# Rounding of the cross-attention tiles spread over ScalarE, VectorE and GpSimd, and started at slots of its own from batch to batch

## Chip, cores and metric

One core of one Trainium2 chip. The metric is the time on the device in microseconds (us) of one launch.

## What is computed

A decoder layer in float32 on 4 batches of 512 tokens, 512 features each: causal attention with 32 query heads and 8 key heads, then a product with a context, then a mixture of experts. Each part has a residual and a layer norm ahead of it. The change is in the second part. There the normalised tokens and the context are rounded to fp8 steps before they are multiplied:

```python
xb = x.reshape(E, M, K // BLK, BLK)            # BLK = 128, here per batch of 512 tokens
amax = jnp.max(jnp.abs(xb), axis=-1, keepdims=True)
safe = jnp.maximum(amax, ACT_EPS)
q = (xb * (FP8_MAX / safe)).astype(jnp.float8_e4m3fn)
xq = q.astype(jnp.float32) * (safe / FP8_MAX)
...
x = x + einsum('emk,enk->emn', xq, wq)         # wq: the context, rounded in blocks of 128 x 128
x = x + shared_ffn(layernorm(x)) + chosen_expert(layernorm(x))
```

## The kernel before

Tokens lie in SBUF as 16 tiles `X[:, t, :]` of 128 tokens by 512 features, four tiles (i = 0 to 3) for each batch b. Products in float32 are made of three matmuls of split operands (`three`, L474 to L476: high by high, high by low, low by high), so nearly every tile that is multiplied is first turned on TensorE (PE; `turn_tile`, L466), copied by ScalarE (ACT; L928) and completed by VectorE (DVE; L1312).

The program has three stages. Attention ends at about 1050 us of the span. The stage from there to about 1317 us is the shared feed-forward network, in 8 half batches x of 256 tokens, each cut into 8 parts k:

- parts 0 to 4 are 24 matmuls of 256 columns (`Uh`, `Ul`), part 5 is 12 of them. After each, ACT applies Silu (L971), DVE multiplies (L1441), and the product is split by ACT (`h_hi`, L958) and DVE (`h_lo`, L1428, L1430);
- part 6 is 30 matmuls of 512 columns (`Dh`, `Dl`), part 7 is 4 of them. Part 6 needs the split products of parts 0 to 4, part 7 that of part 5.

The last stage is the eight experts, with the same parts.

The cross part of batches 1 to 3 and the choice of experts run beside the second stage. `slots()` gives every step a slot; every engine walks the same slots, and ahead of part k of half batch x it runs its share of slot 8x + k - 5. For batch b, s = 16(b - 1), and slot s is the one before part 5 of half batch 2(b - 1). Every engine is a queue in program order: what stands behind a waiting instruction waits too. The steps, before the change, with their slots:

- `stats2` (s - 13 + i) and `norm2` (s - 7): mean, variance and reciprocal root on DVE; `rstd_of` is 11 small operations, L1103 to L1114.
- `cross_round` (s - 1 + i), all on DVE for one tile: normalise X into a tile of `T1` (L1127), largest magnitudes of its four blocks (L1301), the scales (L1232 to L1237), the scaling (L1241), the rounding step (L1247, L1249). GpSimd (POOL) then adds the step, subtracts it, and scales back (L1659, L1661, L1663).
- `cross_turn` (s + 1 + i): turn of the rounded tile. `cross_product` (s + 2 + i): 12 matmuls with the context into bank 6, then DVE adds them to X (`cross_add`, L1317).
- `stats3`, `rstd3` (s + 6), `norm3` (s + 7 + i // 2), `route_turn` (s + 9 + i // 2): the third layer norm, from which the half batches 2b and 2b + 1 of the network start at slot s + 11.
- `logits` (s + 12), `choose` (s + 14), `place` (s + 19, for the last batch s + 15): product with the gate weights, the largest logit by a chain of small DVE operations (L1342 to L1361), the places by two small matmuls (L656, L657) and a second DVE chain (L1370 to L1382). Then POOL numbers the tokens (L1720) and sends four indirect DMAs (L1697).

Batch 0 is done during attention; its `logits`, `choose` and `place` stand at slots -4, -2 and 2. The tiles of `T1` and `T2` are pieces of `work` in the profile. `YT` and `XT` hold turned tokens and the turned context.

Of the kernel before, what the change touches and what calls it, by code (L numbers as in the profile page):

```python
# [5 lines left out]
NT, D, NB, TB = 16, 512, 4, 4  # L6
# [4 lines left out]
NU = NG * NB  # L11
# [24 lines left out]
def slots():  # L36

    side = {}


    def plan(s, stage, b, i=0):
        side.setdefault(s, []).append((stage, b, i))

    first = ("route_turn", "cross_turn", "logits", "choose", "place", "cross_product")
    for i in range(TB):
        plan(-36 + i, "context_turn", 0, i)
        plan(-32 + 2 * i, "cross_turn", 0, i)
        plan(-31 + 2 * i, "cross_product", 0, i)
        plan(-30 + 2 * i, "stats3", 0, i)
        plan(-22 + i, "norm3", 0, i)  # L50
        plan(-20 + i, "route_turn", 0, i)
        plan(-16 + i, "context_turn", 1, i)
    plan(-23, "rstd3", 0)
    plan(-4, "logits", 0)
    plan(-2, "choose", 0)
    plan(2, "place", 0)
    for b in range(1, NB):
        s = 16 * (b - 1)
        for i in range(TB):
            plan(s - 13 + i, "stats2", b, i)  # L60
            if b > 1:
                plan(s - 4 + i + i // 3, "context_turn", b, i)
            plan(s - 1 + i, "cross_round", b, i)
            plan(s + 1 + i, "cross_turn", b, i)
            plan(s + 2 + i, "cross_product", b, i)
            plan(s + 3 + i, "stats3", b, i)
            plan(s + 7 + i // 2, "norm3", b, i)
            plan(s + 9 + i // 2, "route_turn", b, i)
        plan(s - 7, "norm2", b)
        plan(s + 6, "rstd3", b)  # L70
        plan(s + 12, "logits", b)
        plan(s + 14, "choose", b)
        plan(s + (19 if b < NB - 1 else 15), "place", b)
    for i in range(2):
        plan(16 * NB - 13 + i, "load_x", i)
        plan(16 * NB - 9 + i, "expert_turn", 0, i)
    plan(16 * NB - 11, "load_slots", 0)

    def place(x):
        return first.index(x[0]) if x[0] in first else len(first) - 9 * (x[0] == "context_turn")  # L80

    for s in side:
        side[s].sort(key=place)
    return side
# [12 lines left out]
def decoder(nc, x_in, ctx_in, wqkv_in, wo_in, wg_in, wf_in, ident_in, mask_in, rope_in, ksin_in, rank_in, tri_in, out):  # L97
# [3 lines left out]
    with ExitStack() as root:  # L101
# [10 lines left out]
        X = sb("X", [128, NT, D])  # L112
# [202 lines left out]
        def tokens(i):  # L315
            return slice(i * 128, (i + 1) * 128)

        def four(y):
            return y.rearrange("p (c n) -> p c n", c=4)
# [7 lines left out]
        def turned_from(x):  # L327
            stage, b, i = x
            if stage == "context_turn":
                return CW[(4 * b + i) % 3]  # L330
            if stage == "cross_turn":
                return T1[(b * TB + i) % 3]
            return XN[:, i, :] if stage == "route_turn" else XE[:, b % 2, i, :]

        def turn_bank(n):
            return 6 if turns[n] in beside else other_at[turns[n]] % 2

        def wait_job_buffer(need, j):

# [441 lines left out]
        def scalar_engine(e):  # L781
            need = Once(e)
# [104 lines left out]
            def look(t):  # L887
# [4 lines left out]
                e.activation(free_wraw[:, 1024:1536], X[:, t, :], ACT.Identity, bias=ssum[:, 0, t:t + 1],  # L892
                             scale=rstd[:, t:t + 1]).then_inc(a_norm, 1)

            def scaled(j):

                y, k = YB[j % 4], job_scales(j, 0)
                if jobs[j][0] == "context":
                    need.wait_ge(v_small, 2)
                    need.wait_ge(d_rb[j % 4], 16 * sum(x[0] == "context" for x in jobs[j % 4:j + 1:4]))  # L900
                else:
                    need.wait_ge(v_small, 4)
                    need.wait_ge(a_norm, TB + jobs[j][1] + 1)
                for c in range(4):
                    last = e.activation(y[:, tokens(c)], y[:, tokens(c)], ACT.Copy, scale=k[:, c:c + 1])
                last.then_inc(a_scaled, 1)
# [23 lines left out]
            def logits(b):  # L930
                need.wait_ge(p_logits, b + 1)
                if b == 0:
                    wait_attention(need)
                else:
                    need.wait_ge(p_lt, b)
                e.activation(LG[:, :], bank[6][:, :], ACT.Copy).then_inc(a_lg, 1)

            def side_slot(s):
                for x in side.get(s, ()):
                    if x in turn_at:  # L940
                        turn(x)
                    elif x[0] == "logits":
                        logits(x[1])

            def split_piece(m, p):
                n = NP * m + p
# [142 lines left out]
        def vector_engine(e):  # L1089
# [3 lines left out]
            def chain(instruction):  # L1093
                own[0] += 1
                instruction.then_inc(v_own, 1)

            def after():
                need.wait_ge(v_own, own[0])
# [17 lines left out]
            def rstd_of(ts):  # L1116
                chain(rstd_first(ts))
                for _ in range(3):
                    rstd_next(ts)
# [6 lines left out]
            def normed(dst, t):  # L1126
                return e.tensor_scalar(dst, X[:, t, :], mv[:, t, 0:1], rstd[:, t:t + 1], ALU.subtract, ALU.mult)  # L1127
# [108 lines left out]
                chain(e.tensor_scalar(r, r, 448.0, None, ALU.mult))  # L1236
                return e.tensor_scalar(d, d, 1.0 / 448.0, None, ALU.mult)  # L1237

            def rounded(n, y, r):
                q = T2[n % 2]  # L1240
                chain(e.tensor_tensor(four(y), four(y), r.unsqueeze(2).to_broadcast([128, 4, 128]), ALU.mult))  # L1241
                after()
                if n < 2:
                    need.wait_ge(p_kv, NU)
                else:
                    need.wait_ge(g_t2, n - 1)
                chain(e.tensor_scalar(q.bitcast(U32), y.bitcast(U32), 0x7F800000, None, ALU.bitwise_and))  # L1247
                after()
                e.tensor_scalar(q, q, 2.0 ** -6, 1.5 * 2.0 ** 20, ALU.max, ALU.mult).then_inc(v_q, 1)  # L1249
# [36 lines left out]
                need.wait_ge(v_bm, j + 1)  # L1286
                e.tensor_scalar(q, q, 2.0 ** -6, 1.5 * 2.0 ** 20, ALU.max, ALU.mult).then_inc(v_bq, 1)

            def cross_round(b, i):
                t = b * TB + i  # L1290
                y = T1[t % 3]
                if b == 1:
                    need.wait_ge(a_kept, len(jobs))
                    need.wait_ge(v_small, 4)
                need.wait_ge(p_turn, turn_at["cross_turn", (t - 3) // TB, (t - 3) % TB] + 1)
                after()
                chain(normed(y, t))
                after()
                if b > 1:
                    need.wait_ge(g_q, round_at["cross_round", b - 1, i] + 1)  # L1300
                chain(e.tensor_reduce(aam[:, i, :], four(y), AX.X, ALU.max, apply_absolute_value=True))  # L1301
                after()
                chain(scales(aam[:, i, :], asc[:, i, 0, :], asc[:, i, 1, :], 1e-4))
                after()
                rounded(round_at["cross_round", b, i], y, asc[:, i, 0, :])

            def turn_lo(x):
                n = turn_at[x]
# [75 lines left out]
            def side_slot(s):  # L1384
                ends = []
                for x in side.get(s, ()):
                    stage, b, i = x
                    if stage == "stats2":
                        need.wait_ge(v_x, last_x(b * TB + i) + 1)
                        stats_of(b * TB + i)  # L1390
                    elif stage == "stats3":
                        need.wait_ge(v_x2, b * TB + i + 1)
                        stats_of(b * TB + i)
                    elif stage in ("norm2", "rstd3"):
                        rstd_of(slice(b * TB, (b + 1) * TB))
                    elif stage == "cross_round":
                        cross_round(b, i)
                    elif stage == "norm3":
                        norm3(b, i)
                    elif stage == "choose":  # L1400
                        choose(b)
                    elif stage == "place":
                        place(b)
                    elif stage == "expert_turn":
                        turn_lo(x)
                    elif stage == "cross_product" or x in turn_at:
                        ends.append(x)
                for x in ends:
                    if x in turn_at:
                        turn_lo(x)  # L1410
                    else:
                        cross_add(x[1], x[2])
# [179 lines left out]
        def gpsimd_engine(e):  # L1592
# [108 lines left out]
            def side_slot(s):  # L1701
                for x in side.get(s, ()):
                    stage, b, i = x
                    if stage == "cross_round":
                        rounded(round_at[x], T1[(b * TB + i) % 3], asc[:, i, 1, :])
                    elif stage == "place":
                        number(b)
                        scatter(b)
# [421 lines left out]
```

## Time and profile before

| | us |
|---|---|
| median of 3 runs (1546.54 to 1547.84) | 1546.98 |
| the profiled execution, its own time | 1547.13 |
| span of its trace | 1545.3 |
| busy: PE, DVE, POOL, ACT | 1444.7, 1166.0, 1025.9, 960.9 |

The span runs from the first to the last instruction; 1.8 us of the execution's own time lie outside it. Busy time is a sum over the whole span, and each stage has its own limit, so what counts is who waits for whom in the stage that is touched. PE is busy 93% of the span on average, and least in the slices of the second stage.

### The profile page before, as it was taken

The page shows a single profiled execution, that of the slowest core. Times are in us where ns is not written, and L with a number is a line of the kernel's source. Part 1 is how long each engine was busy: PE and PEld are TensorE (multiplying, and loading weights), DVE is VectorE, ACT ScalarE, POOL GpSimd, SP SyncE. Part 2 cuts the span into 40 slices and gives each one's busy share as a digit, 9 for nine tenths or more (in the row PEclk, how much of TensorE's full clock was granted, in tenths as well). Part 3 has the DMA queues.
Part 4 walks back from the last instruction along what each step waited for, and adds up shares of the span by engine and source line. Part 5 has one row for each costly group of instructions (what it writes and reads, how often), then busy time and mean ns, then how long its engine had stood idle before and what let it go on. Part 6 is the DMA issues. An engine that isn't in the chain of part 4 may idle for free.

```text
span 1545.3 us, 26936 instructions
## 1 busy us (share of the span) xinstructions
PE 1444.7 (93%) x8617; PEld 1264.8 (82%) x8617; DVE 1166.0 (75%) x2877; ACT 960.9 (62%) x2446; POOL 1025.9 (66%) x1043
## 2 busy tenths in 40 slices
PE   5999999999999999999999999886989899999997
PEld 4778888888878888778888887765888879999996
DVE  7678888888888887778878888786767664677773
ACT  4677777787677787878888788663121212556562
POOL 3787888887886889888889889443403041366663
PEclk9999999999999999999999999998999999999999
DMA  6445444334231433424334333403111010587772
GB/s 209 128 112 174 137 125 137 98 98 120 75 95 49 128 84 97 122 60 120 95 91 133 90 110 93 130 22 124 42 42 42 21 42 34 167 268 230 254 242 84
DMA packets 108620, 174.74 MB, mean 113 GB/s; under 512 B 20936, under 2 KB 42696, under 8 KB 108480
## 3 DMA queue, kind: packets, MB, share of 16 engines
q1 hardware_dynamic: 104448, 160.51, 35.5%
q0 software_dynamic: 3840, 12.25, 2.1%
q8 instruction: 70, 1.15, 0.3%
q14 instruction: 70, 0.57, 0.1%
q10 hardware_dynamic: 192, 0.26, 0.1%
HBM read 94.05 MB, written 33.18 MB: 82 GB/s over the span
## 4 chain that ended last, share of the span: by engine, by line
PE 66%; DVE 13%; ACT 11%; issue 5%; DMA 2%; POOL 1%; SPq 1%; DVEq 0%; POOLq 0%; ACTq 0%
PE bank L474 15%; PE bank L476 14%; PE bank L475 14%; PE bank L526 5%; ACT P L865 5%; PE bank L541 4%; PE bank L542 4%; PE bank L492 4%; PE bank L493 3%; DVE P L1179 2%; ACT PTh L877 2%; PE bank L466 2%; ACT Otmp L871 2%; DVE PTl L1220 1%; DVE Opair L1214 1%
## 5 line engine op out<-in xcount | busy, mean ns | idle before, releaser
L865 ACT ACTIVATE P<-P,mn 128x512 f32<-128x512 f32 (+3 forms) x512 | 284.6, 557 | 206.3 <-DVE mn L1179 202.3
L1616 POOL TENSOR_TENSOR P<-P,ri 128x128 f32<-128x128 f32 (+3 forms) x512 | 360.1, 735 | 31.1 <-DVE ri L1168 30.8
L1179 DVE CUSTOM_DVE_ANT_0 P<-bank,mask 128x512 f32<-128x512 f32 (+3 forms) x512 | 236.8, 481 | 88.8 <-PE bank L493 87.1
L1220 DVE TENSOR_TENSOR PTl<-bank,PTh 128x512 fp32r<-128x512 f32 (+1 forms) x384 | 229.7, 599 | 33.9 <-ACT PTh L877 31.3
L526 PE MATMUL bank<-ident,P 128*128 128x128 f32 x1280 | 201.8, 272 | 2.5 <-POOL P L1616 2.5
L877 ACT ACTIVATE PTh<-bank 128x512 fp32r<-128x512 f32 (+1 forms) x384 | 197.7, 516 | 3.4 <-PE bank L526 0.5
L492 PE MATMUL bank<-KT,QT 128*128 128x256 f32 (+2 forms) x512 | 188.2, 368 | 6.6 <-DVE mn L1179 6.6
L474 PE MATMUL bank<-XT,Wh 128*128 128x512 f32 x384 | 163.5, 426 | 6.4 <-DVE XT L1150 3.5
L541 PE MATMUL bank<-PTh,VS 128*128 128x256 f32 (+2 forms) x512 | 161.8, 327 | 6.7 <-DVE X L1229 2.4
L493 PE MATMUL bank<-KT,QT 128*128 128x256 f32 (+2 forms) x512 | 165.8, 324 | 0.0
L542 PE MATMUL bank<-PTl,VS 128*128 128x256 f32 (+2 forms) x512 | 155.3, 325 | 0.0
L476 PE MATMUL bank<-XT,Wl 128*128 128x512 f32 x384 | 152.7, 398 | 0.0
L475 PE MATMUL bank<-XT,Wh 128*128 128x512 f32 x384 | 152.4, 397 | 0.0
L526 PEld LDWEIGHTS bank<-ident,P 128*128 128x128 f32 x1280 | 149.4, 141 | 3.0 <-POOL P L1616 3.0
L1654 POOL TENSOR_TENSOR OTl<-Opair,OTh 128x512 fp32r<-128x512 f32 x64 | 83.4, 1303 | 97.9 <-ACT OTh L922 97.0
L474 PE MATMUL bank<-Oh,OTh 128*128 128x512 f32 x256 | 106.2, 415 | 20.5 <-DVE Opair L1214 15.0
L971 ACT ACTIVATE hm<-bank 128x256 f32<-128x256 f32 x96 | 36.3, 378 | 133.6 <-PE bank L476 133.0
L1214 DVE TENSOR_TENSOR Opair<-bank,Otmp 64x512 f32<-64x512 f32 x128 | 87.3, 682 | 38.8 <-ACT Otmp L871 37.6
L492 PEld LDWEIGHTS bank<-KT,QT 128*128 128x128 f32 x512 | 97.0, 189 | 21.4 <-DVE mn L1179 9.1
L541 PEld LDWEIGHTS bank<-PTh,VS 128*128 128x128 f32 x512 | 96.8, 189 | 20.9 <-issue 8.0
L493 PEld LDWEIGHTS bank<-KT,QT 128*128 128x128 f32 x512 | 97.6, 191 | 10.5
L542 PEld LDWEIGHTS bank<-PTl,VS 128*128 128x128 f32 x512 | 96.7, 189 | 10.1
(224 smaller groups left out, 4096.7 us busy)
## 6 DMA issues: line engine op xcount, KB each, us to landing
RW<-in_wf SPq DMA_DIRECT2D x153, 256.0 KB, 3.5
QT<-qh SPq DMA_DIRECT2D x256, 64.0 KB, 2.0
QT<-ql SPq DMA_DIRECT2D x252, 64.0 KB, 2.0
Oraw<-in_wo SPq DMA_DIRECT2D x16, 512.0 KB, 4.7
KT<-KT SPq DMA_DIRECT2D x32, 256.0 KB, 3.0
Wraw<-in_wqkv SPq DMA_DIRECT2D x9, 768.0 KB, 4.8
xnx<-in_ctx SPq DMA_DIRECT2D x24, 256.0 KB, 3.8
saved<-Wh SPq DMA_DIRECT2D x7, 768.0 KB, 3.5
```

The source lines that it names most:

```text
L474: e.matmul(ps, lh, rh, start=start, stop=False)
L475: e.matmul(ps, lh, rl, start=False, stop=False)
L476: return e.matmul(ps, ll, rh, start=False, stop=stop)
L492: e.matmul(ps[:, 0:k], lhs, KT[:, u % 2, 0, 0:k], start=True, stop=False)
L493: e.matmul(ps[:, 0:k], lhs, KT[:, u % 2, 1, 0:k], start=False, stop=True).then_inc(p_s, 1)
L526: last = e.transpose(ps[:, tokens(m)], src, ident[:, :])
L541: e.matmul(ps[:, q:512], lhs, pt_of(PTh, kb), start=kb == 0, stop=False)
L542: last = e.matmul(ps[:, q:512], lhs, pt_of(PTl, kb), start=False, stop=kb == 3)
L865: e.activation(pq, pq, ACT.Exp, bias=mn[:, z, qb:qb + 1], scale=-1.0, accum_out=rs[:, z, qb:qb + 1]).then_inc(a_exp, 1)
L1179: e.tensor_tensor_reduce(P[:, z, off[qb]:off[qb] + k], bank[n % 2][:, 0:k], mask[:, 512 - k:512], -0.125, BIG, ALU.add, ALU.min, mn[:, z, ...
L1220: e.tensor_tensor(pt_part(PTl, part), bank[2 + part][:, 0:128 * n].rearrange("p (m n) -> p m n", n=128), pt_part(PTh, part).bitcast(F32), ...
L1616: e.tensor_tensor(pq, pq, ri[:, z, qb:qb + 1].to_broadcast([128, n]), ALU.mult).then_inc(g_norm, 1)
```

## The change

From batch 1 on, the chain of `cross_round` is cut into steps with slots of their own. ScalarE normalises (`look`), VectorE finds the largest magnitudes (`peaks`) and the scales of all four tiles at once (`scales`), ScalarE scales (`scaled`, four instructions for each tile), VectorE makes the step (`cross_round`, now L1247 and L1249 alone), and GpSimd does its three operations as before. `T1` has three tiles, so the fourth tile is normalised into a tile of `T2` for its maxima, and normalised a second time into the first tile of `T1` once that was turned. `norm2` gets one more small operation, `bias_of`. The steps of a batch start earlier, by more for batches 2 and 3 (d = 1) than for batch 1 (d = 0), and the tiles stand at uneven distances. `place` of a batch moves from s + 19 to s + 14, which is slot s - 2 of the next batch.

```diff
-    plan(-4, "logits", 0)
-    plan(-2, "choose", 0)
-    plan(2, "place", 0)
+    plan(-3, "logits", 0)
+    plan(-1, "choose", 0)
+    plan(1, "place", 0)
     for b in range(1, NB):
         s = 16 * (b - 1)
+        d = 0 if b == 1 else 1
         for i in range(TB):
-            plan(s - 13 + i, "stats2", b, i)
+            plan(s - 13 - 3 * d + i, "stats2", b, i)
+            plan(s - 8 - 2 * d + i, "look", b, i)
+            plan(s - 7 - 2 * d + i, "peaks", b, i)
             if b > 1:
-                plan(s - 4 + i + i // 3, "context_turn", b, i)
-            plan(s - 1 + i, "cross_round", b, i)
-            plan(s + 1 + i, "cross_turn", b, i)
-            plan(s + 2 + i, "cross_product", b, i)
-            plan(s + 3 + i, "stats3", b, i)
-            plan(s + 7 + i // 2, "norm3", b, i)
-            plan(s + 9 + i // 2, "route_turn", b, i)
-        plan(s - 7, "norm2", b)
-        plan(s + 6, "rstd3", b)
-        plan(s + 12, "logits", b)
-        plan(s + 14, "choose", b)
-        plan(s + (19 if b < NB - 1 else 15), "place", b)
+                plan(s - 6 + i, "context_turn", b, i)
+            begin = s + ((-2, -1, 1, 2), (-4, -3, -1, 1))[d][i]
+            turn = s + ((0, 2, 3, 5), (-1, 0, 1, 3))[d][i]
+            product = s + ((2, 3, 4, 6), (0, 1, 2, 4))[d][i]
+            plan(begin - 1, "scaled", b, i)
+            plan(begin, "cross_round", b, i)
+            plan(turn, "cross_turn", b, i)
+            plan(product, "cross_product", b, i)
+            plan(product + 1, "stats3", b, i)
+            plan(s + (8, 6)[d] + d * (i // 2), "norm3", b, i)
+            plan(s + (9, 8)[d] + i // 2, "route_turn", b, i)
+        plan(s - 9 - 3 * d, "norm2", b)
+        plan(s - 4 - 2 * d, "scales", b)
+        plan(s + 7 - 2 * d, "rstd3", b)
+        plan(s + 11 - d, "logits", b)
+        plan(s + 12, "choose", b)
+        plan(s + 14, "place", b)
...
+            def look_later(b, i):
+                need.wait_ge(v_small, 3 + 2 * b)
+                if i == 3:
+                    need.wait_ge(p_kv, NU)
+                    need.wait_ge(g_t2, TB * (b - 1))
+                    normed_by(T2[1], b * TB + i)
+                    return
+                need.wait_ge(p_turn, turn_at["cross_turn", b - 1, i or 3] + 1)
+                normed_by(T1[i], b * TB + i)
+
+            def scaled_later(b, i):
+                y = T1[i % 3]
+                if i == 3:
+                    need.wait_ge(p_turn, turn_at["cross_turn", b, 0] + 1)
+                    normed_by(y, b * TB + i)
+                need.wait_ge(v_small, 4 + 2 * b)
+                need.wait_ge(a_norm, normed_at(b, 4 if i == 3 else i))
+                for c in range(4):
+                    last = e.activation(y[:, tokens(c)], y[:, tokens(c)], ACT.Copy, scale=asc[:, i, 0, c:c + 1])
+                last.then_inc(a_scaled, 1)
...
-            def rounded(n, y, r):
+            def rounded(n, y):
                 q = T2[n % 2]
-                chain(e.tensor_tensor(four(y), four(y), r.unsqueeze(2).to_broadcast([128, 4, 128]), ALU.mult))
-                after()
+                need.wait_ge(a_scaled, len(jobs) + n + 1)
...
-            def cross_round(b, i):
-                t = b * TB + i
-                y = T1[t % 3]
...
-                rounded(round_at["cross_round", b, i], y, asc[:, i, 0, :])
+            def peaks(b, i):
+                need.wait_ge(a_norm, normed_at(b, i))
+                chain(e.tensor_reduce(aam[:, i, :], four(T2[1] if i == 3 else T1[i]), AX.X, ALU.max,
+                                      apply_absolute_value=True))
+
+            def later_scales(b):
+                need.wait_ge(a_kept, len(jobs))
+                need.wait_ge(g_q, TB * (b - 1))
+                after()
+                scales(aam[:, :, :], asc[:, :, 0, :], asc[:, :, 1, :], 1e-4).then_inc(v_small, 1)
```

`look` and `scaled` use `ACT.Identity` (in `normed_by`) and `ACT.Copy`. Within a slot, steps that are not named in the tuple `first` come behind those that are, so `choose` and `place` run ahead of `cross_round` on DVE and POOL.

## Rows read from the trace of the kernel before

**Rows 1.** Windows, batches 2 and 3: PE, PEld, DVE, ACT, POOL busy; clock; DMA; GB/s

```profile
1151.20:1229.20 78.00, 70.31 (x449) 63.44 (x448) 54.59 (x144) 16.40 (x37) 18.97 (x17) 0.96 0.10 35
1229.20:1307.00 77.80, 70.32 (x445) 63.01 (x444) 48.91 (x129) 15.34 (x35) 18.96 (x17) 0.96 0.07 28
```

**Rows 2.** Waits of PE, 1074 to 1320 us: total us, times, longest

```profile
PE bank L466 <- POOL work L1663: 13.7, 3, 6.1
PE bank L474 <- DVE lp L1371: 4.2, 3, 1.4
PE bank L656 <- DVE X L1317: 3.4, 2, 1.8
PE bank L474 <- issue: 2.1, 3, 0.7
```

**Rows 3.** Windows of single parts on PE: length, busy, clock, DMA, GB/s

```profile
1159.68:1167.62 7.94, 7.94 (x32) 0.86 0.00 0
1175.79:1180.06 4.27, 4.27 (x12) 0.63 0.29 107
1191.74:1201.82 10.08, 10.08 (x85) 1.00 0.01 2
1202.61:1209.56 6.95, 6.95 (x33) 1.00 0.00 0
```

**Rows 4.** Timeline of DVE: one tile's rounding, first and last operation; choose; place

```profile
1162.56 1.07 DVE L1127 TENSOR_SCALAR work<-X,mv,rstd 128x512 f32<-128x512 f32 x1
...
1166.26 0.43 DVE L1249 TENSOR_SCALAR work<-work 128x512 f32<-128x512 f32 x1
...
1147.57 0.19 DVE L1342 COPY lg<-bank 128x32 f32<-128x32 f32 x1
...
1149.23 0.77 DVE L1361 TENSOR_TENSOR cum<-cum,lq 128x8 bf16<-128x8 bf16 x4
...
1175.14 0.41 DVE L1370 COPY cum<-cum 128x8 bf16<-128x8 bf16 x1
...
1177.16 0.17 DVE L1382 CAST sidx<-sm 128x4 uint32<-128x4 f32 x1
```

**Rows 5.** Timeline of POOL: one tile, first and last; numbering and last scatter

```profile
1160.62 1.28 POOL L1659 TENSOR_TENSOR work<-work 128x512 f32<-128x512 f32 x1 [1.82 <-DVE work L1249]
...
1163.41 1.11 POOL L1663 TENSOR_TENSOR work<-work,asc 128x512 f32<-128x512 f32 x1
...
1177.42 0.20 POOL L1720 TENSOR_SCALAR XN<-code 128x4 f32<-128x4 f32 x1 [0.78 <-DVE sidx L1382]
...
1182.31 0.97 POOL L1697 DMA_INDIRECT xd<-XN,sidx  x1 [0.30 <-issue]
```

**Rows 6.** A DVE split beside POOL; all of POOL's L1659 (min/median/max ns)

```profile
1161.05 1.13 DVE L1428 TENSOR_TENSOR Hl<-hm,Hh 128x256 fp32r<-128x256 f32 x1
...
L1659 POOL TENSOR_TENSOR work<-work x12: 1268/1292/1392, 1077.9 to 1250.8; 128x512 f32<-128x512 f32 x12
```

**Rows 7.** ScalarE: Silu, normalising, four scalings of a tile, table loads

```profile
L971 ACT ACTIVATE hm<-bank 128x256 f32<-128x256 f32 x96 | 36.3, 378 | 133.6 <-PE bank L476 133.0
...
L892 ACT ACTIVATE Wraw<-X,ssum,rstd 128x512 f32<-128x512 f32 x4 | 3.2, 805 | 0.0
...
689.69 1.27 ACT L905 ACTIVATE xnx<-xnx,asc 128x128 f32<-128x128 f32 x4
...
L971 ACT ACT_TABLE_LOAD x2 | 2.6, 1283 | 0.0
```

**Rows 8.** The start of the stage: PE's wait, POOL's split ahead of it, norm2

```profile
1057.02 0.77 PE L474 MATMUL bank<-XT,Gh 128*128 128x512 f32 x1 [4.15 <-issue]
...
1056.67 0.25 POOL L1812 TENSOR_TENSOR Gl<-Graw,Gh 128x32 fp32r<-128x32 f32 x1
...
1050.39 0.67 DVE L1103 TENSOR_SCALAR mv<-mv 128x4 f32<-128x4 f32 x1
...
1052.87 0.16 DVE L1114 SCALAR_TENSOR_TENSOR rstd<-rtmp,rstd 128x4 f32<-128x4 f32 x1
```

More of the change, by code:

```diff
@@ L331, in turned_from @@
             if stage == "cross_turn":
-                return T1[(b * TB + i) % 3]
+                return T1[i % 3]
             return XN[:, i, :] if stage == "route_turn" else XE[:, b % 2, i, :]
@@ L336, in turn_bank, with normed_at @@
             return 6 if turns[n] in beside else other_at[turns[n]] % 2
+        def normed_at(b, i):
+            return TB + TB + 5 * (b - 1) + i + 1
         def wait_job_buffer(need, j):
@@ L893, in look, with normed_by @@
                              scale=rstd[:, t:t + 1]).then_inc(a_norm, 1)
+            def normed_by(dst, t):
+                e.activation(dst, X[:, t, :], ACT.Identity, bias=ssum[:, 0, t:t + 1],
+                             scale=rstd[:, t:t + 1]).then_inc(a_norm, 1)
+            def look_later(b, i):
[17 more added lines that the diff above has]
+                last.then_inc(a_scaled, 1)
             def scaled(j):
@@ L943, in side_slot @@
                         logits(x[1])
+                    elif x[0] == "look":
+                        look_later(x[1], x[2])
+                    elif x[0] == "scaled":
+                        scaled_later(x[1], x[2])
             def split_piece(m, p):
@@ L1287, in large_steps_of, with bias_of @@
                 e.tensor_scalar(q, q, 2.0 ** -6, 1.5 * 2.0 ** 20, ALU.max, ALU.mult).then_inc(v_bq, 1)
-            def cross_round(b, i):
-                t = b * TB + i
-                y = T1[t % 3]
[L1292 to L1295, printed above, removed]
-                after()
-                chain(normed(y, t))
-                after()
[L1299 to L1304, printed above, removed]
-                rounded(round_at["cross_round", b, i], y, asc[:, i, 0, :])
+            def bias_of(b):
+                ts = slice(b * TB, b * TB + TB)
+                after()
+                e.scalar_tensor_tensor(ssum[:, 0, ts], mv[:, ts, 0], -1.0, rstd[:, ts], ALU.mult,
+                                       ALU.mult).then_inc(v_small, 1)
+            def peaks(b, i):
[5 more added lines that the diff above has]
+                need.wait_ge(g_q, TB * (b - 1))
+                after()
+                scales(aam[:, :, :], asc[:, :, 0, :], asc[:, :, 1, :], 1e-4).then_inc(v_small, 1)
             def turn_lo(x):
@@ L1395, in side_slot @@
                         rstd_of(slice(b * TB, (b + 1) * TB))
+                        if stage == "norm2":
+                            bias_of(b)
+                    elif stage == "peaks":
+                        peaks(b, i)
+                    elif stage == "scales":
+                        later_scales(b)
                     elif stage == "cross_round":
-                        cross_round(b, i)
+                        rounded(round_at[x], T1[i % 3])
                     elif stage == "norm3":
@@ L1704, in side_slot @@
                     if stage == "cross_round":
-                        rounded(round_at[x], T1[(b * TB + i) % 3], asc[:, i, 1, :])
+                        rounded(round_at[x], T1[i % 3], asc[:, i, 1, :])
                     elif stage == "place":
```

## The prediction, made before the run

> **What bounds the kernel now.** I read the page first, then the windows of the second stage, then who waits for whom in it. In the windows PE is the fullest engine, but it stands still for about 7.6 us in each stretch of 78 us, and the granted clock is 0.96, though DVE is busy for only 55 us of it and POOL for 19 [rows 1]. The waits of PE say where: three long ones for the last POOL operation of a rounded tile, then short ones for DVE in the same places, 23.4 us together over the three batches [rows 2]. The windows of single parts show the clock after such waits. Part 6, 6.95 us at the full clock of 2.4 GHz, took 7.94 at a granted 0.86 behind a wait of nearly 4 us, and the twelve matmuls of a cross product took 4.27 at 0.63, in part at 1.2 GHz [rows 3]. A mean of 0.96 over 78 us is a loss of 3.1 us. Per batch that is 7.8 + 3.1 = 10.9 us, for the three about 33 us. It bounds what better order can bring in this stage.
>
> The cause stands in the timeline of DVE. One tile's rounding holds it from 1162.56 to 1166.69, 4.1 us, and four follow each other with the splits of parts 4 to 6 queued between them [rows 4]. POOL then takes from 1160.62 to 1164.52, 3.9 us [rows 5]. PE has too little work until the first tile arrives.
>
> **Durations used.** At full clock 84 matmuls of parts 0 to 4 took 10.08 us: 2.88 for a part, 1.44 for part 5. Part 6 is 6.95, so a cross product (12 of its 30) is 2.8. Between the ends and beginnings in those rows, 1201.82 to 1202.61, lie two turned tiles: 0.4 each [rows 3]. The chain of choose is 2.4 us (1147.57 to 1150.0), place 2.2 (1175.14 to 1177.33) [rows 4]. Numbering and four scatters hold POOL from 1177.42 to 1183.28, 5.9 us [rows 5]. DVE reaches a slot about 1.0 us behind PE, my estimate from Silu at 0.38 [rows 7], a product of about its size and the handovers.
>
> **What is removed and added.** DVE loses per tile the normalising, the scaling and the scales, 2.5 to 3.5 us of 4.1 or more; the maxima and two operations of 0.43 stay. That is some 12 us per batch, and it stood in front of PE. ACT gains 0.8 for a normalising and 1.27 for four scalings, per batch 5 x 0.8 + 4 x 1.27 = 9.1 us [rows 7], on an engine busy 16 of 78 us [rows 1]: hidden, as each lies one or more parts of 2.88 ahead of its reader. Were this cover gone, it would be 1 to 2 us in front of a split. POOL's work is unchanged. SP's loads of context tiles follow context_turn, now earlier and three slots apart: nothing. The second normalising of tile 3 stands behind the turn of tile 0 on ACT, and its round two parts later: nothing.
>
> No row shows Identity beside Silu. From below it costs no load; from above two loads of 1.28 around each. I take none, since Identity already runs between exponentials and Copy between Silus, and the trace has two loads at Silu in all [rows 7]. The Trainium skill ("ScalarE: Activation LUTs", section "Table sets: the hidden batching unit") says identity and copy are in every set; by it the price is nil, and no run here shows it yet.
>
> **POOL becomes the last, batches 2 and 3.** Count from PE's begin of slot s - 4. Until the turn of tile 2 (slot s + 1) PE has parts 1 to 4 (11.5), part 5 (1.4), one product (2.8) and five turns (2.0): 17.7 us. On DVE choose stands ahead of the first tile: 1.0 + 2.4 + 0.9 = 4.3, when POOL can begin. POOL does tile 0, tile 1, then place of the batch before (slot s - 2), then tile 2: 3 x 3.9 + 5.9 = 17.6. So tile 2 is done at 21.9, and PE waits 4.2 us.
>
> To this comes what DVE and POOL do to each other. A split on DVE that takes 0.4 took 1.13 when it began inside a POOL operation, and it ended 0.28 behind that one's end (1161.90); POOL's own operation rose from 1268 to at most 1392 ns [rows 5, 6]. The Trainium skill ("SBUF — State Buffer", section "Who interferes with whom") says that the two hold one port pair in turn, for a whole instruction, where DVE copies, does a tensor_scalar or reads two tiles from SBUF; by it each such operation beside POOL waits for an end of POOL's. The row agrees for DVE. Now the splits, the chain of place and the second and third rounding run beside a busy POOL, where before POOL waited for most of them. Walking the queue with up to one POOL operation of delay each, place's result comes at about 13.4 instead of 10.5, numbering starts there and not at 12.1, the split of turned tile 0 comes at 15.6 (a first wait of PE, 2.2), and tile 2 at 23.6. Together 5.7 us. Bounds: 0, if POOL were ahead; 10.9, all that is lost now. I take 5.7, nearest to the rows. For batch 2 the last product waits some 0.7 more behind statistics of the next batch on DVE. Two waits again lower the clock: 2.3 us, between 0 and the present 3.1. Route turns in slots s + 8 and s + 9 remove the wait of 0.7 that PE has each time for the last of them. Sum: batch 2 now 10.9, then 8.7 to 9.0: gain 1.9; batch 3, without the 0.7: gain 2.8.
>
> **Batch 1 and the start.** Logits of batch 0 now stand behind part 1. PE waited 4.15 us for the gate weights' last split on POOL, done at 1056.9 [rows 8]; part 1 (2.88) fills that. But ACT's look waits for norm2, 2.6 us on DVE [rows 8], and three looks then stand ahead of the last splits of weights and of the gate weights: logits start 1.3 later. Gain here 1.6. In the chain, choose moved to slot -1 and tile 0 reaches PE after a wait of 1.5 instead of 6.1, and the clock falls less: gain 6.5. Place of batch 0 stands on POOL ahead of tile 2 in slot 1 here too: from part 6 PE has 6.95 + 0.4 + 2.8 + 0.9 = 11.1, POOL with DVE's lag and place ahead 3.3 + 5.9 + 3.9 = 13.1, later by the delays of choose and place: a wait of 4.1, where two of 1.4 stood: loss 1.3 (and 0.4 of a delayed part 6). Norm3 of all four tiles in slot 8, one slot behind rstd3, makes the first route turn wait 2.0 more: rstd3 and statistics (3.1), maxima, splits and the first norm against 7.2 of PE. Sum: 1.6 + 6.5 - 1.3 - 2.0 = 4.8, as no further clock loss is taken.
>
> Total 4.8 + 1.9 + 2.8 = 9.5 us. The sum is against the profiled execution, 1547.13 (span 1545.3 and 1.8 around it); the median is 0.15 below. That gives 1537.5. The experts start earlier by as much and take as long as before.
>
> **Rivals.** First, **the chain is hidden**: scatters or rounding hold POOL for less than the rows show, or PE's side work covers the rest. For it: DVE, the cause now, loses most of its share. Against it: the sum of POOL, which needs no guess. It would give 33 less the wait of 0.7 left in batch 1, and 2.7 at the start: 1547.1 - 35 = 1512; half hidden about 1524. Chance 0.20, spread over 1512 to 1530.
>
> Second, **the wait only changes its name**: the delays of DVE beside POOL double, waits of about 8 us stand again in each batch and the clock falls as now, and the start brings nothing. Then 1544 to 1550, typically 1547. For it: 22 us of POOL per batch in one block, with some 20 us of DVE beside it. Chance 0.15.
>
> Third, **slower, as POOL is held up too**: beside a busy DVE it also waits, for a whole DVE instruction of 0.43 us [rows 4], at some 14 of them ahead of tile 2. That is 6 us per batch, 18 in all: 1537.5 + 18 = 1555. It decides the sign from about 0.23 us per operation (9.5 / 42). Against it: POOL's worst is 0.12 above its least [rows 6]. Chance 0.07. The same rule of the Trainium skill ("SBUF — State Buffer", section "Who interferes with whom") would have it so, as it blocks whichever engine comes second. Reloads of tables at every Identity (15 times 2.6 on ACT, some of it hidden) would also end near 1555: 0.03.
>
> That the steps are not done ahead, because their engine gets there late, is in the second case.
>
> **How the numbers follow.** The forecast has 0.55, its own range 1530 to 1544. The rivals have 0.20, 0.15 and 0.10. For 8 in 10 the range takes the forecast's (nearly all of 0.55), the half-hidden upper part of the first rival, and the lower half of the second: 1520 to 1547. Something over 0.2% (3.1 us, about what a measurement of this kernel tells from no change) faster: all but 0.04 of the forecast, the first rival and some of the second, 0.77. Within it 0.14, slower 0.09.
>
> **What the changed profile would show.** No wait of PE of over 2 us for tile 0 in batches 2 and 3. A wait of 3 to 6 us at the turn of tile 2 in slot s + 1, released by L1663, with POOL busy without a gap from the first tile through the scatters. DVE busy about 43 us in 70 to 76, ACT about 25. Windows from one batch to the next of 75 to 77 us. Four table loads as before, two at Silu. Small DVE operations and splits of 0.4 to 1.4 us beside POOL. Wrong would be: no wait at tile 2 (the first rival), or DVE still ahead of PE at every turn (the second), POOL's L1659 well over 1.4 us (the third).

## The result

The changed kernel takes 1536.35 us (median of 4 runs, 1535.28 to 1536.89), the kernel before 1547.41 beside it: a ratio of 0.9927, interval 0.9914 to 0.9939, or 11 us less. The forecast was 1537.5. The profiled execution took 1536.31 us with a span of 1534.5.

From part 0 of half batch 2 to part 0 of half batch 4, and from there to that of half batch 6, it is now 74.3 and 72.9 us; before it was 78.1 and 77.8. Two context turns, 0.8 us of TensorE's work, have moved out of the second stretch and ahead of the first, so at equal work the two batches gained 3.8 and 4.1 us. Two windows of 74.0 us, with the columns of rows 1:

```profile
1131.50:1205.50 74.00, 68.82 (x445) 62.15 (x444) 48.86 (x123) 23.77 (x58) 19.37 (x17) 0.98 0.12 40
1205.50:1279.50 74.00, 68.79 (x447) 62.27 (x446) 41.24 (x95) 21.57 (x54) 19.37 (x17) 0.98 0.09 33
```

DVE has lost about 6 us of work in the first and 8 in the second, less than the 12 of the prediction. The instructions that went took 10.6 us per batch (31.7 in all three), and those that stayed got longer: over the stage the 24 operations of the rounding steps (L1289 and L1291 now) went from 10.2 to 14.7 us, the 35 full splits of `h_lo` (L1475 now) from 16.0 to 21.4. ACT has gained 6 to 7, and the clock costs 1.5 us where it cost 3.1. The waits of PE in the stage, 1050 to 1312 us of the changed kernel, against rows 2:

```profile
PE bank L479 <- POOL work L1710: 13.2, 4, 4.0
PE bank L487 <- issue: 3.6, 1, 3.6
PE bank L487 <- ACT YT L967: 1.5, 1, 1.5
PE bank L479 <- DVE XN L1170: 1.4, 1, 1.4
PE bank L487 <- ACT XT L967: 1.3, 1, 1.3
PE bank L479 <- ACT YT L967: 1.0, 1, 1.0
```

POOL's last operation (L1663 before, L1710 now) is still what PE waits for most. But three of the four waits, 4.0, 3.75 and 3.7 us, are now for tile 2. The timeline of POOL in batch 2, with the first operation of tile 0, the numbering, the last scatter and the last operation of tile 2, and PE's turn behind it:

```profile
1142.26 1.29 POOL L1706 TENSOR_TENSOR work<-work 128x512 f32<-128x512 f32 x1 [47.15 <-DVE work L1291]
...
1151.15 0.29 POOL L1767 TENSOR_SCALAR XN<-code 128x4 f32<-128x4 f32 x1 [0.78 <-DVE sidx L1423]
...
1156.29 0.97 POOL L1744 DMA_INDIRECT xd<-XN,sidx  x1 [0.30 <-issue]
...
1160.06 1.30 POOL L1710 TENSOR_TENSOR work<-work,asc 128x512 f32<-128x512 f32 x1
...
1161.41 1.12 PE L479 MATMUL bank<-ident,work 128*128 128x128 f32 x4 [3.75 <-POOL work L1710]
```

Slot s - 4 began on PE at 1137.87. Counted from there POOL began at 4.4 (forecast 4.3), the numbering at 13.3 (13.4), and the turn of tile 2 was free at 23.5 (23.6). TensorE's own work up to that turn took 18.4 us (17.7).

DVE beside this busy POOL: the two operations of tile 1's rounding step, the split behind them, the copy and the first tensor_scalar of place's chain, and a later split. The ACT line stands ahead of the copy of turned tile 0 on ScalarE: it waited 2.11 us for DVE's product, which stood behind that chain, and so PE's first cross product came late.

```profile
1144.09 1.18 DVE L1289 TENSOR_SCALAR work<-work 128x512 uint32<-128x512 uint32 x1
1145.31 1.15 DVE L1291 TENSOR_SCALAR work<-work 128x512 f32<-128x512 f32 x1
...
1146.97 1.12 DVE L1475 TENSOR_TENSOR Hl<-hm,Hh 128x256 fp32r<-128x256 f32 x1
...
1148.35 0.92 DVE L1411 COPY cum<-cum 128x8 bf16<-128x8 bf16 x1
...
1149.62 0.77 DVE L1416 TENSOR_SCALAR kp<-sm 128x4 f32<-128x4 f32 x1
...
1151.75 0.42 ACT L1001 ACTIVATE Hh<-hm 128x256 fp32r<-128x256 f32 x1 [2.11 <-DVE hm L1488]
...
1156.87 1.99 DVE L1475 TENSOR_TENSOR Hl<-hm,Hh 128x256 fp32r<-128x256 f32 x1
```

### The profile page after: what moved, and what is told of

It reads as the page before. It is cut to its first block, busy times and chain, and to the rows that moved or that the text cites. A ratio compares the mean times of both kernels' runs of the same rounds, so it can differ in the third digit from the quotient of the medians.

```text
span 1534.5 us, 26939 instructions
## 1 busy us (share of the span) xinstructions
PE 1439.9 (94%) x8617; PEld 1260.9 (82%) x8617; DVE 1146.9 (75%) x2820; ACT 984.9 (64%) x2509; POOL 1026.8 (67%) x1043
## 3 DMA queue, kind: packets, MB, share of 16 engines
q8 instruction: 70, 1.15, 0.3%
## 4 chain that ended last, share of the span: by engine, by line
PE 64%; ACT 12%; DVE 11%; issue 6%; POOL 3%; DMA 2%; SPq 1%; DVEq 0%; POOLq 0%; ACTq 0%
PE bank L487 14%; PE bank L489 14%; PE bank L488 14%; PE bank L539 5%; ACT P L878 5%; PE bank L554 3%; PE bank L555 3%; PE bank L505 3%; PE bank L506 3%; DVE P L1222 2%; ACT PTh L890 2%; PE bank L479 2%; ACT Otmp L884 2%; DVE PTl L1263 2%; DVE Opair L1257 1%
## 5 line engine op out<-in xcount | busy, mean ns | idle before, releaser
L1663 POOL TENSOR_TENSOR P<-P,ri 128x128 f32<-128x128 f32 (+3 forms) x512 | 359.9, 734 | 32.2 <-DVE ri L1211 32.2
L1762 POOL TENSOR_TENSOR Ul<-RW,Uh 128x512 fp32r<-128x512 f32 x45 | 59.7, 1329 | 66.4 <-ACT Uh L992 66.3
```

The costliest lines, as they stand in the source:

```text
L1663: e.tensor_tensor(pq, pq, ri[:, z, qb:qb + 1].to_broadcast([128, n]), ALU.mult).then_inc(g_norm, 1)
```

## Experiments

Each is an edit of the changed kernel. Ratios are against the kernel before, timed on the same chip beside it. Where the length of the stage is given, it runs from its first part 0 to the part 6 of its last half batch, in the one profile of that kernel: 259.6 us before, 249.3 in the changed kernel. What follows took 235.9 to 236.0 us in every profile, so what is not in the stage lies in attention ahead of it. There the stage began anywhere from 1047.1 to 1053.1 us in the ten profiles of kernels that share the changed kernel's attention, so a few us between two medians need not come from the edit.

**1. Place four slots later.** POOL then has all four tiles ahead of the scatters.

```diff
-    plan(1, "place", 0)
+    plan(3, "place", 0)
...
-        plan(s + 14, "place", b)
+        plan(s + (18 if b < NB - 1 else 14), "place", b)
```

> The changed kernel with place of a batch four slots later (s + 18 for batches 1 and 2, slot 3 for batch 0), so that the four scatters stand on POOL behind all four tiles and not ahead of tile 2. Theory (POOL's queue: scatters of 5.5 to 6 us in front of tile 2 make the waits of 4.0, 3.8 and 3.7 us at its turn): these waits are gone, and with them the slow product behind each; PE waits under 1.5 us in those places, 1523 to 1528 us. Rival (DVE beside a busy POOL is what is late, the scatters only happen to stand there): the wait goes to DVE or ScalarE at the same turn or the next product, 1533 to 1537 us.

1517.52 us (0.981, 0.9789 to 0.983), better than expected. PE's waits in the stage:

```profile
PE bank L487 <- issue: 4.0, 3, 3.5
PE bank L487 <- DVE lp L1412: 1.9, 3, 1.0
PE bank L479 <- POOL work L1710: 1.7, 1, 1.7
PE bank L479 <- DVE XN L1170: 1.4, 1, 1.4
PE bank L479 <- ACT YT L967: 1.0, 1, 1.0
```

The only wait for POOL left is that of tile 0 in batch 1. From part 0 of half batch 2 to that of 4, and on to that of 6, it is 68.2 and 66.9 us. In a window of 70.0 us there PE stands still for 0.7, and the clock is at 1.00:

```profile
1125.00:1195.00 70.00, 69.31 (x454) 62.51 (x453) 47.95 (x124) 25.14 (x59) 19.04 (x17) 1.00 0.14 44
```

The stage took 232.0 us, 17.3 less than in the changed kernel. The three waits make 11.5 of that, those of 1.3 and 1.5 at the first products 2.4 (0.15 and 0.3 stay), and the clock that no longer falls behind them about 5.5. On the other side stand three new waits for place's result at its new slot (L1412), 1.9 us in all.

**2. The same slots for every batch.**

```diff
-        d = 0 if b == 1 else 1
+        d = 0
```

> The changed kernel with the slots of batch 1 (d = 0) for batches 2 and 3 as well, place left at s + 14. Theory (POOL is last, and the later start leaves the same POOL block ahead of tile 2, but its turn is two slots later; norm3 in one slot makes the first route turn late): the wait for tile 2 stays near 4 us or goes below it, a wait of 1.5 to 2.5 us at the route turns appears in batches 2 and 3, and 1537 to 1543 us. Rival (starting two parts ahead is what brings the gain of batches 2 and 3): waits of over 3 us for tile 0 come back, 1543 to 1547 us.

1550.11 us (1.0021, 1.0012 to 1.0031): above both expectations and slower than before. With d = 0 the first tile is rounded in slot s - 2, and there place of the batch before comes ahead of it on POOL:

```profile
1147.12 0.30 POOL L1767 TENSOR_SCALAR XN<-code 128x4 f32<-128x4 f32 x1 [54.72 <-DVE sidx L1423]
...
1153.35 1.29 POOL L1706 TENSOR_TENSOR work<-work 128x512 f32<-128x512 f32 x1
...
1157.24 1.09 PE L479 MATMUL bank<-ident,work 128*128 128x128 f32 x4 [6.45 <-POOL work L1710]
```

The waits of 1.5 to 2.5 us that were expected at the route turns came out at 3.2, 3.1 and 0.8. So this run mixed two things, the start and the neighbour of place. Experiment 4 separates them.

**3. Old slots, new engines.** Begin s - 1 + i, turn s + 1 + i, product s + 2 + i, rstd3 s + 6, norm3 s + 7 + i // 2, route turns s + 9 + i // 2, logits s + 12, choose s + 14, place s + 19 or s + 15, and batch 0's at -4, -2 and 2:

```diff
-            begin = s + ((-2, -1, 1, 2), (-4, -3, -1, 1))[d][i]
-            turn = s + ((0, 2, 3, 5), (-1, 0, 1, 3))[d][i]
-            product = s + ((2, 3, 4, 6), (0, 1, 2, 4))[d][i]
+            begin = s - 1 + i
+            turn = s + 1 + i
+            product = s + 2 + i
```

> The changed kernel with the work spread over the three engines, but the slots of rounding, turn, product, norm3, route turn, logits, choose and place as they were in the kernel before. Theory (DVE's 4 us per tile were the cause, and place at its new slot costs waits of 4 us): the first tile makes PE wait about 0.7 us instead of 3.8 and 6.1, the later ones hardly, no wait of 4 us for tile 2, 1522 to 1530 us, so below the changed kernel. Rival (the spread alone brings little, the early start brings the gain): waits of over 3 us for tile 0 stay, 1540 to 1546 us.

1527.58 us (0.9874, 0.9858 to 0.989), in the theory's range and 9 us below the changed kernel; the stage took 243.1 us. The waits for tile 0 were longer than expected. In batches 2 and 3 they fell from 3.8 us to 1.5 and 1.6, twice the 0.7 expected, with choose ahead of tile 0 on DVE. In batch 1 the wait fell from 6.1 to 3.4 only, which is over the 3 us that the rival names. And tile 3 of batch 1 waits 1.1 us, for place of batch 0 stands between tiles 2 and 3 on POOL there:

```profile
1081.06 1.04 PE L479 MATMUL bank<-ident,work 128*128 128x128 f32 x4 [3.38 <-POOL work L1710]
...
1102.22 0.66 PE L479 MATMUL bank<-ident,work 128*128 128x128 f32 x4 [1.12 <-POOL work L1710]
...
1154.53 0.63 PE L479 MATMUL bank<-ident,work 128*128 128x128 f32 x4 [1.49 <-POOL work L1710]
```

**4. The same slots, with place late.** Experiments 1 and 2 together.

> Place four slots later as in the run with place late (1517.5 us), and the slots of batch 1 (d = 0) for batches 2 and 3 as well. Theory (in the run with the same start the wait of 6.5 us for tile 0 came from place, which then stood ahead of tile 0 on POOL): that wait is gone, and what is left of the later start is the route turns' wait of 3.2 and 1.0 us in batches 2 and 3: 1523 to 1529 us. Rival (the early start itself removes the wait for tile 0): a wait of over 3 us for tile 0 stays, 1533 to 1545 us.

1529.72 us (0.9889, 0.9873 to 0.9904), just above the theory's range. No wait for tile 0 is left in batches 2 and 3, but the first route turn waits there:

```profile
PE bank L479 <- DVE XN L1170: 7.1, 3, 3.2
```

Against experiment 1 (1517.52) that is 12 us, though not by the wait for tile 0. In the profiles the stage took 241.3 us against 232.0, so the early start is worth 9.3 us there; attention ended 4 us later in this run's profile, for which I have no cause.

**5. POOL's third operation cut to 4 columns** (the scaling back of the other 508 is left out).

```diff
-                e.tensor_tensor(four(y), four(y), d.unsqueeze(2).to_broadcast([128, 4, 128]), ALU.mult).then_inc(g_q, 1)
+                e.tensor_tensor(four(y)[:, :, 0:1], four(y)[:, :, 0:1], d.unsqueeze(2), ALU.mult).then_inc(g_q, 1)
```

> The changed kernel, where POOL's third operation of a tile scales back only 4 columns of the 512, the first of each block (the scaling back of the others is left out). It takes about 0.25 us instead of 1.04. Theory (the length of POOL's queue up to tile 2 sets PE's wait): three tiles ahead of that turn are 2.2 to 2.4 us shorter, the waits fall from 3.7 to 4.0 us to about 1.5, 1526 to 1531 us. Rival (DVE is late): the waits keep their length within 0.5 us, 1534 to 1537 us.

1527.44 us (0.9868, 0.9846 to 0.9889). The time is the theory's, its wait is not: 2.9 us stand at tile 2, not 1.5.

```profile
1156.00 0.66 PE L479 MATMUL bank<-ident,work 128*128 128x128 f32 x4 [2.93 <-POOL work L1710]
```

But the wait of 1.34 ahead of the first product is gone, so PE arrives sooner. The two together fell from 5.1 to 2.9 us, by 2.2, nearly the 2.5 us by which the three operations got shorter (1.04 to 0.20 each).

**6. Only POOL's share of place later.** PE and DVE keep slot s + 14; numbering and scatters get a step of their own at s + 18 (slot 3 for batch 0).

```diff
+        plan(s + (18 if b < NB - 1 else 14), "scatter", b)
...
-                    elif stage == "place":
+                    elif stage == "scatter":
                         number(b)
                         scatter(b)
```

> The changed kernel with place where the change puts it on PE and DVE, but POOL's numbering and scatters alone four slots later. Theory (POOL's queue): the waits of 3.7 to 4.0 us at tile 2 are gone, those of 1.3 and 1.5 us at the first product of batches 2 and 3 stay, as DVE's chain of place still stands ahead of the split of turned tile 0: 1519 to 1524 us. Rival (DVE's chain of place is what delays tile 2): the waits at tile 2 stay at 2 us or more, 1529 to 1536 us.

1519.81 us (0.9832, 0.9814 to 0.985). The waits at tile 2 are gone, those at the first product stand:

```profile
1147.94 0.47 PE L489 MATMUL bank<-XT 128*128 128x512 f32 x1 [1.38 <-ACT XT L969]
...
1216.79 0.47 PE L489 MATMUL bank<-XT,YT 128*128 128x512 f32 x1 [1.52 <-ACT YT L969]
```

The stage took 232.6 us, 16.7 less than in the changed kernel and 0.6 more than in experiment 1. So nearly all of experiment 1's gain is POOL's queue. The 2.3 us between the two medians are within what the runs scatter (1518.23 to 1522.79 here, 1516.25 to 1520.12 there).

**7. All three POOL operations cut to 4 columns** (rounding and scaling back of the rest are left out), scatters in their place.

```diff
-                e.tensor_tensor(y, y, q, ALU.add).then_inc(g_own, 1)
+                e.tensor_tensor(y[:, 0:4], y[:, 0:4], q[:, 0:4], ALU.add).then_inc(g_own, 1)
```

and so for the other two.

> The changed kernel where all three POOL operations of a tile work on 4 columns only (rounding and scaling back of the rest are left out); the scatters stay where they are. Theory (beside a busy POOL each copy, tensor_scalar and SBUF-SBUF tensor_tensor of DVE waits for POOL's end, and this is what makes PE wait 1.3 and 1.5 us at the first product): DVE's rounding steps and splits in that stretch, 1.1 to 1.2 us in the changed kernel, fall back to 0.43, both those waits go, and the waits for tile 2 go as well: 1516 to 1520 us. Rival (DVE and ScalarE are late there by their own queues): the 1.3 to 1.5 us waits stay while those for tile 2 go, 1519 to 1524 us.

1514.32 us (0.9798, 0.9782 to 0.9814), the stage 226.6. Both kinds of waits went, and so did those for tile 0 of batch 1. DVE's eight rounding steps of batches 2 and 3 (min/median/max ns), here and in the changed kernel:

```profile
L1291 DVE TENSOR_SCALAR work<-work x8: 426/427/431, 1131.1 to 1214.6; 128x512 f32<-128x512 f32 x8
```

```profile
L1291 DVE TENSOR_SCALAR work<-work x8: 426/786/1146, 1141.8 to 1234.8; 128x512 f32<-128x512 f32 x8
```

The same instruction on the same tile got longer only with POOL's full operations beside it.

**8. Place two slots later**, between tile 2 and tile 3 on POOL (`plan(s + 16, ...)`, slot 2 for batch 0).

> The changed kernel with place only two slots later (s + 16, slot 2 for batch 0), so between tile 2 and tile 3 on POOL. Theory (only what stands ahead of tile 2 counts, tile 3 has time): as with place four slots later, 1516 to 1521 us. Rival (any scatter between the tiles costs): a wait of over 2 us moves to tile 3, 1524 to 1532 us.

1524.27 us (0.986, 0.9839 to 0.9881): a time at the lower end of the rival's range, but neither mechanism. Nothing waits for tile 2 or 3, but the first product does, for DVE's read of place's result:

```profile
1146.81 0.47 PE L487 MATMUL bank<-XT 128*128 128x512 f32 x1 [2.42 <-DVE lp L1412]
```

Place and product share bank 6. In slot s + 16 place stands right ahead of the first product. Its copy and that read (L1411, L1412) stand on DVE behind a rounding step and splits beside a busy POOL, and the copy itself took 0.90 us. The product behind the wait of 2.4 us took 4.4 us at a granted 0.63, and it was the same in batch 3 behind 2.6. What takes place off POOL's path puts it on the bank's.

**9. Batch 1 closer**, on top of experiment 1: turn and product of tile 3 and rstd3 one slot earlier, norm3 in slots 7 and 8.

```diff
-            turn = s + ((0, 2, 3, 5), (-1, 0, 1, 3))[d][i]
-            product = s + ((2, 3, 4, 6), (0, 1, 2, 4))[d][i]
+            turn = s + ((0, 2, 3, 4), (-1, 0, 1, 3))[d][i]
+            product = s + ((2, 3, 4, 5), (0, 1, 2, 4))[d][i]
```

> Place late (1517.5 us), and in batch 1 the turn and product of tile 3 and rstd3 one slot earlier, norm3 of two tiles each in slots 7 and 8. Theory (norm3 of four tiles one slot behind rstd3 makes the route turns wait 1.4 and 1.0 us): both waits gone, nothing new, as tile 3 was ready 10 us ahead of its turn: 1514 to 1516.5 us. Rival (the splits behind norm3 get late instead): 1517 to 1519 us.

1518.6 us (0.9819, 0.9805 to 0.9833), against 1517.52 without it: no difference that these runs tell, and a median in the rival's range. The wait of 1.4 us for norm3 is gone from the profile, and the stage took 230.2 us against 232.0, which is the theory's way. The wait of 1.0 stays. It isn't norm3's: a context turn stands in that slot ahead of the two route turns now, and the third turn waits for ScalarE's copy of an earlier one:

```profile
1121.28 0.60 PE L479 MATMUL bank<-ident,work 128*128 128x128 f32 x4
1121.72 0.60 PE L479 MATMUL bank<-ident,XN 128*128 128x128 f32 x4
1123.34 0.63 PE L479 MATMUL bank<-ident,XN 128*128 128x128 f32 x4 [1.02 <-ACT YT L967]
```

By the medians the experiment is inconclusive.

**10. The head earlier**, on top of that: batch 1's stats2 in slots -18 to -15, norm2 in -14, look from -13, peaks from -12.

> As the run with batch 1 closer, and the statistics, norm2, normalising for the maxima (look) and maxima of batch 1 some five slots earlier, inside the end of attention. Theory (the looks on ScalarE behind norm2 delay the gate weights' split by 1.3 us, which PE waits for at the first logits): that wait falls from 3.5 to about 2.2 us, 1 to 1.5 us less than the run before it. Rival (the looks hold up the last heads instead): the stage starts later by as much, no difference or 1 us more.

1517.46 us (0.9814, 0.98 to 0.9828). The wait of 3.5 us at the first logits vanished altogether, but the end of attention holds a longer one than the 2.3 of the other runs, and the stage begins some 6 us later, though it is 3.2 us shorter (227.0):

```profile
1048.69 0.50 PE L487 MATMUL bank<-Oh,OTh 128*128 128x512 f32 x1 [4.16 <-DVE X L1272]
```

That fits the rival, the work only moved. Since experiment 4's profile also began the stage 4 us later without this edit, how much is due to it stays open.

No version that computes everything was measured clearly below experiment 1, 29 us below the kernel before and 19 below the change. Experiments 6, 9 and 10 can't be told apart from it.

## Why the prediction was right

**The cause.** DVE's 4 us per tile made most of the waits for tile 0. Experiment 3 shows it nearly by itself: with the engines changed and, of what was there before, only statistics, norm2 and context turns earlier, 19 us are gained and the three waits fall from 13.7 to 6.5 us. What is left of them, 3.4 us in batch 1, was not traced by a run of its own.

**POOL becomes the last.** The forecast of 5.7 us of waits in batch 2 was 5.1, in two places, as forecast. (The prediction's own 23.6 - 17.7 is 5.9.) POOL's queue ended when it was forecast to; the waits are shorter since TensorE's own work ahead of that turn took 18.4 us. Experiments 1 and 6 show that the scatters ahead of tile 2 make the larger wait, experiment 5 that a shorter queue of POOL shortens it nearly one for one. Experiment 7 shows that the smaller comes from DVE's waits beside POOL, experiments 1 and 6 that it also needs place's chain in that spot on DVE: without either, 0.3 us or less is left. The prediction's walk through the queue had DVE's waits as up to one POOL operation each. Most rows have that; the split of 1.99 us, 1.57 over its 0.42, is longer than any operation of POOL. The trace agrees with the Trainium skill ("SBUF — State Buffer", section "Who interferes with whom") that a tensor_scalar, a copy and a tensor_tensor with both inputs in SBUF wait on DVE for POOL's end, 0.43 us becoming 1.15. Against the third rival, that POOL is held up as much, stand its rows in the stage: L1706 took at most 1416 ns where 1268 is its least, and L1710 at most 1297 where 1038 is its least, in two of its twelve.

**ScalarE.** No wait of PE in the stage was traced to the scalings or normalisings: those of 1.3 and 1.5 us behind ACT go back to DVE, that of 1.0 to three turns in one slot. With 15 normalisings and 48 scalings among the Silus the trace still has two table loads at Silu, as the Trainium skill has it ("ScalarE: Activation LUTs", section "Table sets: the hidden batching unit"):

```profile
L1014 ACT ACT_TABLE_LOAD x2 | 2.6, 1283 | 0.0
```

**Where the sizes were off.** The parts of the sum erred in opposite ways, so that 10.8 us came out near the 9.5 is in part luck. Batches 2 and 3 gained 3.8 and 4.1 us, not 1.9 and 2.8: waits 0.5 shorter, 1.5 us of lost clock instead of 2.3, and in batch 2 no wait of 0.7 for the last product. That leaves 10.8 - 7.9 = 2.9 us for what lies ahead, and 0.5 of them were there when the stage began (1049.81 before, 1049.29 now), which no part of the sum had. So start and batch 1 gained 2.4 us, not 4.8. The waits had the sizes forecast: 1.7 for tile 0 (1.5), 4.0 for tile 2 (4.1), 1.4 and 1.0 at the route turns (2.7 in all), though the 1.0 comes from the context turn beside them (experiment 9) and not from norm3. Part 2 began 13.9 us behind part 0 instead of 15.3, a gain of 1.4 (1.6). The term that was mis-sized is the last of that paragraph, "as no further clock loss is taken". Behind the wait of 4.0 us the turn took 0.4 us longer, and the product 4.80 us at a granted 0.56, so mostly at 1.2 GHz, instead of 2.8. The windows of that product in batches 1, 2 and 3, with what follows it in part:

```profile
1092.22:1097.02 4.80, 4.80 (x15) 0.56 0.00 0
1162.18:1166.20 4.02, 4.02 (x14) 0.68 0.00 0
1236.16:1240.59 4.43, 4.43 (x16) 0.61 0.00 0
```

Those 2.4 us are the difference. The first rival, the chain hidden at about 1512, did not come by the change, but place stood in most of its way: with it moved, experiment 1 reaches 1517.5.

## What to carry to other kernels

When work leaves the engine that is last, write out the queue of the one that gets or keeps it, in order, with everything that shares it: here three tiles and four scatters, 17.6 us against 17.7 of TensorE's work up to that turn and 4.3 of lead lost. The gain of a better split can be eaten by a neighbour in that queue that was moved along with it, or by the bank that it shares, so try the neighbour in more than one slot. A wait of TensorE of 3.7 to 4.0 us cost 1.4 to 2.4 us more in the turn and the work behind it here, one of 2.4 to 2.6 us (experiment 8) 1.6; those of 1.3 and 1.5 us at the first products of the changed kernel cost nothing more.

## What was not expected of the hardware

That the engines hold each other up so unequally: beside POOL an operation of DVE went from 0.43 to 1.15 us and from 0.16 to 0.92 (L1411, with POOL's operations cut short and in the changed kernel), while POOL's own rose by 0.26 at most in the stage. That largest rise stands in the rows of the result, the 1.30 us of L1710, and what DVE did beside it shows the order: the rounding step L1289 had begun 0.01 us earlier and kept its own length, POOL's operation paid, and the next of DVE, begun inside POOL's, paid in turn:

```profile
1160.05 0.41 DVE L1289 TENSOR_SCALAR work<-work 128x512 uint32<-128x512 uint32 x1
1160.49 1.14 DVE L1291 TENSOR_SCALAR work<-work 128x512 f32<-128x512 f32 x1
```

The page cited above describes both sides alike, and these rows agree. My reading of the inequality, not tested by itself, is that DVE's short instructions fall inside POOL's long ones far more often than the other way round.

And kernels with the same attention code ended attention up to 6 us apart in their profiles (the stage began at 1047.1 in experiment 7, 1048.8 in experiment 1 and 1053.1 in experiment 4), as much as some of the effects sought here. What makes this difference stays open.
